# Attention and the second layer's norm, gate, dispatch and shared expert in one stage of interleaved steps

## The reference

```python
x = x + 0.5 * ffn(layernorm(x))      # weights of one layer, used twice
x = x + attn(layernorm(x))
x = x + 0.5 * ffn(layernorm(x))

def attn(x):                         # 16 heads of 8 values
    q, k, v = x @ Wq + bq, x @ Wk + bk, x @ Wv + bv
    q, k = elu(q) + 1.0, elu(k) + 1.0
    kv = einsum('bhnd,bhnf->bhdf', k, v)
    return einsum('bhnd,bhdf->bhnf', q, kv) @ Wp + bp

def ffn(x):                          # 16 experts of 176, the best two of a token, and a shared one of 352
    scores = softmax(x @ gate_w + gate_b)
    y = sum over the best two e of score_e * ((silu(x @ w1[e] + b1[e]) * (x @ w3[e] + b3[e])) @ w2[e] + b2[e])
    z = (silu(x @ sw1 + sb1) * (x @ sw3 + sb3)) @ sw2 + sb2
    return y + z
```

## Time and profile before

| | us |
|---|---|
| median of 3 runs | 1020.25 |
| profiled execution | 1019.16 |
| its span on the core | 1017.4 |
| attention, from its first load to its last add | 424.7 to 566.9 |
| second front stage, to the first load of the second experts | 566.9 to 780.5 |

### The profile page before, as it was taken

One profiled execution on the slowest core, in us unless ns is written; L12 is line 12 of the kernel. 1 busy time (PEld: TensorE's weight loads), 2 busy tenths in 40 slices (PEclk: granted clock), 3 DMA queues, 4 the chain that ended last, 5 costly groups with the idle time before them and its releaser, 6 DMA issues. The chain is left out here.

```text
span 1017.4 us, 20412 instructions
## 1 busy us (share of the span) xinstructions
PE 800.3 (79%) x5408; PEld 717.5 (71%) x5409; DVE 588.2 (58%) x1989; ACT 468.7 (46%) x926; POOL 590.6 (58%) x600
## 2 busy tenths in 40 slices
PE   2899999709999999238988389988841999999920
PEld 2678787609999999237777378877741999999920
DVE  5677776505555555167875477766621555555536
ACT  3466665205555555145564256556310555555510
POOL 2457777745777777533320146777774577777740
PEclk9899999959999999759999579989975999999965
DMA  9912221323333333331100001111132233333349
GB/s 275 133 47 70 66 64 51 85 71 85 101 104 102 101 104 97 117 123 58 67 1 1 1 22 35 52 48 51 51 95 68 78 101 104 99 102 104 97 155 371
DMA packets 82819, 90.42 MB, mean 89 GB/s; under 512 B 20414, under 2 KB 69451, under 8 KB 80715
## 3 DMA queue, kind: packets, MB, share of 16 engines
q1 hardware_dynamic: 63052, 45.42, 17.4%
q0 software_dynamic: 17408, 35.95, 10.7%
q10 hardware_dynamic: 2304, 8.39, 2.1%
HBM read 47.46 MB, written 44.37 MB: 90 GB/s over the span
## 5 line engine op out<-in xcount | busy, mean ns | idle before, releaser
L873 POOL DMA_INDIRECT ys<-e_y,e_x x288 | 275.8, 958 | 130.9 <-issue 88.9
L316 POOL DMA_INDIRECT xs<-f_xrow,f_slot x256 | 252.8, 987 | 82.5 <-issue 75.4
L992 PE MATMUL e_py<-w,e_at 97*128 (+1 forms) x1152 | 152.1, 274 | 0.0
L992 PEld LDWEIGHTS e_py<-w,e_at 97*128 97x128 f32 (+1 forms) x1152 | 139.9, 191 | 0.1
L897 DVE TENSOR_TENSOR e_a<-e_pu,e_sil 128x352 f32<-128x352 f32 x144 | 75.5, 524 | 97.3 <-ACT e_sil L923 92.3
L904 DVE TENSOR_SCALAR e_y<-e_py,e_x 128x128 f32<-128x128 f32 x288 | 87.8, 346 | 57.9 <-PE e_py L992 57.6
L917 ACT ACTIVATE e_xth<-e_px 128x256 fp32r<-128x256 f32 x144 | 55.2, 384 | 142.2 <-PE e_px L956 142.2
L649 ACT ACTIVATE f_sil<-f_phg,sb 128x512 f32<-128x512 f32 (+1 forms) x96 | 64.7, 685 | 100.0 <-PE f_phg L742 99.6
L756 PEld LDWEIGHTS f_pz<-sw,f_gated 128*128 128x128 f32 (+1 forms) x768 | 103.5, 197 | 9.2
L468 DVE SCALAR_TENSOR_TENSOR f_gated<-f_phg,sb,f_sil 128x512 f32<-128x512 f32 (+1 forms) x96 | 71.7, 747 | 63.4 <-ACT f_sil L649 52.9
L923 ACT ACTIVATE e_sil<-e_pu 128x352 f32<-128x352 f32 x144 | 66.7, 463 | 90.4 <-PE e_pu L969 90.4
(11 more groups left out here) (160 smaller groups left out, 1424.0 us busy)
## 6 DMA issues: line engine op xcount, KB each, us to landing
e_x<-xs SPq DMA_DIRECT2D x288, 65.0 KB
t_yt<-ys SPq DMA_DIRECT2D x8, 1024.0 KB, 4.8
c_yt<-ys SPq DMA_DIRECT2D x8, 1024.0 KB, 10.4
ys<-e_y,e_x POOLq DMA_INDIRECT x288, 2.3
xa<-in_attn_x ACTq DMA_DIRECT2D x8, 512.0 KB, 10.2
xs<-f_xrow,f_slot POOLq DMA_INDIRECT x256, 2.3
out<-xa ACTq DMA_DIRECT2D x8, 512.0 KB
f_raw<-in_ffn_w SPq DMA_DIRECT2D x32, 88.0 KB
```

What stands on the lines that cost most here:

```text
L316: pool.indirect_dma_start(xs, bass.IndirectOffsetOnAxis(slot[:, q, i:i + 1], 0), xrow[:, i, :], None).then_inc(done, 16)
L873: pool.indirect_dma_start(ys, bass.IndirectOffsetOnAxis(xin[r][:, t, D:D + 1].bitcast(I32), 0), y[r][:, t, :], None).then_inc(sent[r], 16)
L992: last = pe.matmul(p_y[r][:, t * D:(t + 1) * D], at[r][0:rows_, q], w2, start=c == 0, stop=c == 1, skip_group_check=True)
```

## The change

`attention` is gone as a stage. Its work is put into `front` with n = 1, by chunks instead of whole groups. A step s there has attention of group s+2, the norm for the feed-forward layer of group s+1, the gate of s and the shared expert of s-1; the residual sum and attention's norm run one group further ahead. Steps run from -3 to 9. The shared expert of n = 1 gets two p_hg buffers, one p_z and two xth and xtl instead of three, two and three, since attention takes three PSUM banks: p_r0, p_r1 and p_b. A p_r bank serves queries, keys and values of two tiles, and the result in turn.

The feature map is taken as max(min(exp(y), 1), y + 1): one exponential with a bias of -1 on ScalarE and one instruction on VectorE that takes the minimum and the maximum. For this y + 1 is what TensorE makes: Wq, Wk, Wv are centred at the end of `front` with n = 0 (two matmuls of 384 columns) and carry the biases and that one, since the transposed rows are copied out with 1 added. The bias matmuls of keys and values and the Relu go.

```diff
@@ build
-        attention(nc, k, sb, ps, xa, ys_v)
-        front(nc, k, sb, ps, 1, xa, xs_dram)
+        front(nc, k, sb, ps, 1, xa, xs_dram, ys=ys_v)
@@ front
+        NH, NZ, NX = (3, 2, 3) if n == 0 else (2, 1, 2)
...
+                if n == 1:
+                    for c in range(CHUNKS):
+                        wait(sp, x2r, c - 3)
+                        sp.dma_start(yt[c % 4][:], ys[:, c // 2, c % 2 * CHUNK:(c % 2 + 1) * CHUNK]
+                                     ).then_inc(y_in[c % 4], 16)
...
+                    sum_y(0)
+                    for s in range(-3, GROUPS + 2):
+                        first(s - 1)
+                        if 0 <= s + 1 < GROUPS:
+                            scales(s + 1)
+                        sum_y(s + 4)
+                        if s + 3 < GROUPS:
+                            scales_a(s + 3)
+                        second_choice(s - 2)
...
+                def phi_q(g, h):
+                    dve.wait_ge(eqr, 2 * g + h + 1)
+                    dve.scalar_tensor_tensor(phq[h][:], phq[h][:], 1.0, p_r[h][:], ALU.min,
+                                             ALU.max).then_inc(qmr, 1)
...
+                def step_1(s):                      # VectorE
+                    a, b, f, m = s + 2, s + 3, s + 1, 6 * (s - 1)
+                    attending, norming, gating = (0 <= g < GROUPS for g in (a, f, s))
+                    if attending:
+                        shifts_a(a)
+                    if norming:
+                        moments(f)
+                        variances(f)
+                    if gating:
+                        largest(s)
+                    gates(m)
+                    if gating:
+                        indices(s)
...
+                    gates(m + 1)
+                    outs(2 * (s - 1) - 1)
+                    if b < GROUPS:
+                        residual(b)
+                    gates(m + 2)
+                    if 0 <= s - 2 < GROUPS:
+                        rewrite(s - 2)
+                    if b < GROUPS:
+                        moments_a(b)
+                    gates(m + 3)
...
+                    if b < GROUPS:
+                        variances_a(b)
+                    if norming:
+                        shifts(f)
+                    gates(m + 4)
+                    outs(2 * (s - 1))
+                    if gating:
+                        hot(s)
+                    gates(m + 5)
+                    if gating:
+                        low(2 * s)
+                    if attending:
+                        phi_q(a, 0)
+                        phi_q(a, 1)
+                        phi_k(a, 0)
+                        phi_k(a, 1)
+                    if gating:
+                        sums(s)
+                    if attending:
+                        phi_k(a, 2)
+                        phi_k(a, 3)
+                    if gating:
+                        places(s)
+                    if attending:
+                        heads_only(a)
+                    if gating:
+                        low(2 * s + 1)
+                    if attending:
+                        attended(a, 0)
+                        attended(a, 1)
...
+                def exp_k(g, r):
+                    both = p_r[r % 2][:].rearrange("p (t n) -> p t n", n=2 * D)
+                    act.wait_ge(kvmm, 4 * g + r + 1)
+                    wait(act, vtkr, 4 * g + r - 1)
+                    act.activation(v[r % 2][:], both[:, :, D:2 * D], ACT.Copy)
+                    act.activation(phk[r % 2][:], both[:, :, 0:D], ACT.Exp, bias=k.minus1[:]
+                                   ).then_inc(ekr, 1)
...
+                def queries(g, h):
+                    pe.wait_ge(xtr, place_of["attention", 2 * g + h] + 1)
+                    wait(pe, x3r, 2 * (g - 1) + h + 1)
+                    pe.matmul(p_r[h][:], k.wqkv[:, 0:D], xt_a[h][:], start=True, stop=True
+                              ).then_inc(qmm, 1)
+
+                def keys(g, r):
+                    if r < 2:
+                        pe.wait_ge(qmr, 2 * g + r + 1)
+                    else:
+                        pe.wait_ge(kvmr, 4 * g + r - 1)
+                    for i in range(2):
...
+                        last = pe.matmul(p_r[r % 2][:, i * 2 * D:(i + 1) * 2 * D],
+                                         xt_a[r // 2][:, q * P:(q + 1) * P], k.wqkv[:, D:3 * D],
+                                         start=True, stop=True)
+                    last.then_inc(kvmm, 1)
```

More of the change, by code:

```diff
@@ L324, in scales, with first @@
                                        ).then_inc(rstd, 1)
[L326 to L340, removed]
+                def first(g):
+                    if not 0 <= g < GROUPS:
+                        return
+                    pool.wait_ge(slots, g + 1)
+                    pool.wait_ge(weighted, g + 1)
+                    pool.wait_ge(xhr, 2 * g + 2)
+                    pool.sem_inc(passed, 1)
+                    send(g, 0, sent0[g % 3])
@@ new lines, in second_choice, with sum_y @@
+                def second_choice(g):
+                    if not 0 <= g < GROUPS:
+                        return
+                    pool.wait_ge(rewrote, g + 1)
+                    pool.sem_inc(passed, 1)
+                    send(g, 1, sent1)
+                def sum_y(g):
+                    if not 0 <= g < GROUPS:
+                        return
+                    for c in (2 * g, 2 * g + 1):
+                        y = yt[c % 4]
+                        pool.wait_ge(y_in[c % 4], 16 * (c // 4 + 1))
+                        pool.tensor_tensor(y[:, :, 0:D], y[:, :, 0:D], y[:, :, D:2 * D], ALU.add
+                                           ).then_inc(ysum, 1)
@@ new lines, in scales_a @@
+                def scales_a(g):
+                    pool.wait_ge(var_a, g + 1)
+                    wait(pool, xhr_a, 2 * (g - 1))
+                    pool.tensor_tensor(rs_a[g % 2][:], ve_a[:], k.nhalf[:], ALU.pow
+                                       ).then_inc(rstd_a, 1)
+                if n == 0:
+                    for g in range(3):
+                        scales(g)
+                    for g in range(GROUPS + 1):
+                        first(g)
+                        if g + 3 < GROUPS:
+                            scales(g + 3)
+                        second_choice(g - 1)
+                else:
[8 more added lines that the diff above has]
+                        second_choice(s - 2)
@@ L682, in _ @@
                 if n == 0:
+                    step(-1)
+                    step(0)
                     act.wait_ge(sw_in, 32)
@@ new lines, in values_keys, with project @@
+                def values_keys(g, r):
+                    pe.wait_ge(kvmr, 4 * g + r + 1)
+                    if r == 0:
+                        wait(pe, kvpr, g)
+                    for i in range(2):
+                        last = pe.matmul(p_b[:, 0:D], v[r % 2][:, i], phk[r % 2][:, i],
+                                         start=r == 0 and i == 0, stop=r == 3 and i == 1)
+                    last.then_inc(vtkr, 1)
+                def project(g):
+                    pe.wait_ge(kvtr, g + 1)
+                    pe.matmul(p_b[:, D:2 * D], kvt[:], k.wp[:], start=True, stop=True
+                              ).then_inc(kvpmm, 1)
@@ new lines, in _ @@
+                    pe.wait_ge(rest_in, 16 * REST)
+                    pe.wait_ge(blo, 1)
+                    pe.wait_ge(wlo, E)
+                    pe.matmul(p_w[:, 0:3 * D], k.centre[:], rawq[:], start=True, stop=False)
+                    pe.matmul(p_w[:, 0:3 * D], k.part[:], rowq[:], start=False, stop=True
+                              ).then_inc(wmean, 1)
+                    step(GROUPS + 1)
+                else:
+                    for s in range(-3, GROUPS + 2):
+                        step_1(s)
```

530 lines of the change are left out of this document (246 added, 284 removed).

## The result

The changed kernel takes 1006.42 us (median of 4 runs, 1004.89 to 1007.08), the kernel before 1020.9 us in the same session: a ratio of 0.9858, 95% interval 0.9835 to 0.9882. The forecast was 1017 us, its range 988 to 1040. The side is right and the range holds, but the gain is 14 us where 3 were forecast, so some terms of the sum are wrong. The profiled execution took 1006.99 us, its span 1005.3.

The account below looks back on a forecast made before the run. Attention and second front (355.8 us) were taken as paced per group, the front's end by GpSimd's sends. Interleaved: 12.3 + 83.6 + 180.5 + 42.6 + 30.3 + 4.0 = 353.3 us, so 1017 us; range 988 to 1040.

Parts of the forecast that it names:

- the head: Step s = -3, from the stage's first load at 424.7 to the first shift, with half-group loads and sums: 12.3 us.
- the starting steps: Steps s = -2, -1, 0, with no shared expert beside them: 72.6 us at full clock, 94 at half, 83.6 taken.
- the full steps: Steps s = 1 to 5, attention, norm, gate and shared expert of four groups: 36.1 us each, 180.5 for five.
- The walk: A full step's three successive stretches, counted from TensorE's gate to the last attends: 34.5 us, before extras.
- The port: GpSimd's sums hold VectorE's residuals: 0.8 us a full step; as a rival, held in full, 1030 us, chance 0.07.
- (a): Full step's first stretch, gate start to last gated product: VectorE the longest, to 18.0 us, TensorE's 16.9 beside it.
- The sign given for being wrong: Attention's matmuls run between the shared expert's waits, so that TensorE is 90% busy in full steps.
- The chain through ScalarE and two buffers: In full steps, attention's chain follows the shared expert's on three in-order engines and two p_r buffers; groups cost more.
- the first rival: Engines overlap further, TensorE running ahead through the waits: full steps of 31 us, 991 us in all; chance 0.28.
- The sends do spread: GpSimd has slack in full steps: 42.6 us to the last slots, 24 sends left in 30.3, 4.0 to next load.
- The rival that kept 16 sends back: GpSimd's root scales_a, waiting ahead of second_choice, keeps 16 sends for the end: 20 us, 1037 us; chance 0.04.
- the half clock through (c): Rival: TensorE at half clock through a full step's attention chain, exp_q to attends: 20 us more, 1037 us; chance 0.15.

Follow-up runs that it names:

- a filled wait: Changed kernel with six idle matmuls of 512 columns between the queries and the keys of each full step: 1004.98 us, ratio 0.9849.

## Why the forecast was right in kind and wrong in size

The range holds and the side is right, but not safely: the time lies at the lower edge of the forecast's own case (1006 to 1028 us), in which same had a larger chance (0.45) than faster (0.40). By stretch the errors are +1.3 us in the head, -7.8 in the starting steps, -5.6 in the full steps, +1.3 from there to the next load, and +1.2 outside the stage.

- **Head.** 13.6 us instead of 12.3: its pair of residuals took 3.40 us beside the sums, 2.1 more than alone.
- **Starting steps: mis-sized by 7.8 us.** 21.5, 25.3 and 29.0 us are 75.8, where 83.6 was taken as the middle of 72.6 at full clock and 94 at half clock (the middle is 83.3). The granted clock, 0.76 to 0.80, was not as low as in the rows that the forecast went by (0.65 and 0.52). These are the stretches at half clock:

```profile
440.40:449.86 9.46, 5.46 (x12) 2.60 (x12) 6.57 (x21) 6.24 (x12) 4.02 (x3) 0.50 0.34 113
463.51:470.34 6.83, 5.43 (x12) 2.60 (x12) 5.43 (x31) 3.74 (x9) 5.34 (x4) 0.50 0.47 154
473.75:477.17 3.42, 3.08 (x7) 2.52 (x8) 1.07 (x3) 0.89 (x3) 0.00 (x0) 0.50 0.00 0
490.82:504.47 13.65, 6.31 (x19) 3.25 (x20) 9.40 (x49) 6.19 (x15) 5.63 (x4) 0.50 0.22 77
```

Of TensorE's 50.9 busy us in the three steps 20.3 lie in them. Four transposes take 1.12 us in them and 0.60 at full clock, so by this estimate the half clock can have cost some 10 us at most, not the 21.4 between 72.6 and 94: "every matmul of the chain at half clock" was the wrong upper end to average with. A part was hidden besides: the first transposes (443.40 to 444.52) ran beside ScalarE's row scalings (441.70 to 444.89). What the half clock cost in fact, and with it whether 72.6 was right, stays open: no run had these steps at full clock.
- **Full steps: mis-sized by 5.6 us** (174.9 instead of 180.5), by errors that partly cancel. The walk: 32.9 us where it said 34.5. With a filled wait the gate starts at 619.88, the query's exponential at 639.93, 20.05 us on (forecast 21.4); from there to the last attended rows are 13.7 us (13.1); and the next gate starts 0.9 us before these end, which the walk did not take off. The port (VectorE held by GpSimd's work): 6.9 us in three steps where 0.8 in each of five, 4.0, was taken; the root next to the sums had not been counted. The clock: 3.5 us in three falls where 4.0 was taken (1.0 in each of the last two steps, and 1.5 in that of 586, if its stall cost what that of 551 did).
- **In (a), VectorE was named the longest; it is TensorE.** VectorE's list was near enough, but TensorE's 16.9 us "beside it" are the longer ones: in the fifth step, from its gate to its queries, it is idle 0.15 us:

```profile
656.00:675.20 19.20, 19.05 (x126) 15.84 (x124) 13.28 (x64) 13.44 (x27) 13.24 (x13) 1.00 0.14 43
```

  The sign given for being wrong, TensorE 90% busy in a full step, is met in two steps of five (30.65 of 33.9 us), for this and for the half clock, which lengthens its busy time, not because attention's matmuls run between the shared expert's.
- **The chain through ScalarE and two buffers** was right: the edit that starts it earlier is worth 13.6 us, falls of the clock included. That is also why the first rival (31 us a step, 991 us) did not come about by itself: it came, at 31.4 us, once the exponentials stood first and the sums elsewhere.
- **The port, as a rule.** The hold showed in every full step with sums; in the starting step s = -1 the residuals came before the sums and took 1.29 us. The Trainium skill ("SBUF — State Buffer", Who interferes with whom), by which such an instruction waits for a whole GpSimd instruction and a step could pay 2.4 us, was nearer than the 0.8 taken: the rows give 2.9 us of VectorE and 1.9 to 2.6 us of the step. The same section of the Trainium skill also counts copies, casts and `tensor_scalar` among the instructions that can contend with GpSimd, under conditions; the 3.12 us weights and the 2.31 us cast agree.
- **The sends do spread.** 42.5, 31.1 and 4.6 us against 42.6, 30.3 and 4.0: these terms were right, and the 15.1 us by which the stage's end is shorter than before are more than the whole gain. The rival that kept 16 sends back is refuted, and the half clock through (c) too: no full step's mean is under 0.95.

## What to carry to other kernels

When two stages are interleaved, each engine's program is one queue: look at what stands ahead of the first instruction of the other stage's serial chain, since moving 2.8 us of row scalings, a copy and the gate's exponentials behind it won nearly as much here as the whole change. Take passes out of that chain first: one pass less was worth more inside it than in the stage where it had run alone. Place GpSimd's SBUF work by what VectorE does at that time, not by when its data is there: pinned beside moments it cost nothing, free-running it held a two-operand add in one order and a small scaling or a cast in the other.

## What the runs showed of the hardware that was not expected

- A stall and a fall of the clock can stand in for one another: taking 2.9 us of stall out of VectorE won 0.8 us of a step, since a fall of 1.0 us then lay in it and the weights were held; without falls the same stall was worth 1.9 to 2.6 us.
- A 128 x 8 scaling on VectorE, 0.17 us, took 3.12 us beside two GpSimd sums, and a cast of 16 columns 2.31 us beside them; eight moments beside a sum took their usual 1.64 us.
- 14.80 us of idle matmuls did not keep the clock over a wait of 3.00 us.
- A residual on VectorE that started 1.1 us into GpSimd's root was held not by the root alone but by the two sums behind it as well: 3.58 us instead of some 0.65.
